# Writing out the gather and scatter loop of a mixture-of-experts kernel, with the scatter first in each step

## The reference

```python
x = x + attn(layernorm(x), w_qkv, w_out, decay_param)   # x: 2 x 1024 tokens of 512
x = x + ffn(layernorm(x), gate_w, w_gate, w_up, w_down, sw_gate, sw_up, sw_down)

# ffn: 8 experts of hidden size 352, two per token, and a shared expert of 704
scores = softmax(x @ gate_w)
topk_w, topk_idx = top_k(scores, 2)
routed = for each token: sum over its 2 experts of  topk_w * (silu(x @ w_gate[e]) * (x @ w_up[e])) @ w_down[e]
shared = silu(x @ sw_gate) * (x @ sw_up) @ sw_down
out = routed + shared
```

## Time and profile before

| what | us |
|---|---|
| median of 3 runs | 743.88 (741.69 to 747.67) |
| the profiled execution, its own time | 742.37 |
| its span, first to last instruction | 740.4 |
| PE busy in the span | 658.0 (89%) |
| DVE busy | 441.3 (60%) |
| ACT busy | 235.9 (32%) |
| POOL busy | 232.0 (31%) |
| mean granted PE clock | 0.967 |

### The profile page before, as it was taken

One profiled execution on the slowest core, in us unless ns is written; L12 is line 12 of the kernel. 1 busy time (PEld: TensorE's weight loads), 2 busy tenths in 40 slices (PEclk: granted clock), 3 DMA queues, 4 the chain that ended last, 5 costly groups with the idle time before them and its releaser, 6 DMA issues. The chain is left out here.

```text
span 740.4 us, 11819 instructions
## 1 busy us (share of the span) xinstructions
PE 658.0 (89%) x3677; PEld 424.2 (57%) x3678; DVE 441.3 (60%) x808; ACT 235.9 (32%) x353; POOL 232.0 (31%) x312
## 2 busy tenths in 40 slices
PE   3989889779899698899998999999999999999971
PEld 2757577558577365465655656655555555555540
DVE  6879878987997661687876976432333332233320
ACT  4244421242342222446665665411111111111110
POOL 6100110101102026333432343145444444443421
PEclk9999999999999899899999999999999999999995
DMA  6830012511342577875856315387986788897643
GB/s 214 289 116 15 15 30 72 163 37 45 113 100 78 129 192 198 263 178 150 182 150 147 57 29 86 61 138 130 114 133 128 121 122 115 121 124 128 106 66 42
DMA packets 111234, 86.86 MB, mean 117 GB/s; under 512 B 79280, under 2 KB 86448, under 8 KB 111200
## 3 DMA queue, kind: packets, MB, share of 16 engines
q1 hardware_dynamic: 88848, 43.94, 26.2%
q0 software_dynamic: 12272, 27.34, 22.9%
q10 hardware_dynamic: 10080, 15.14, 6.8%
HBM read 44.45 MB, written 23.33 MB: 92 GB/s over the span
## 5 line engine op out<-in xcount | busy, mean ns | idle before, releaser
L1298 DVE TENSOR_TENSOR hidT<-turn_h,hidT 128x384 f16<-128x384 f32 x71 | 39.4, 555 | 118.5 <-ACT hidT L1047 118.3
L381 PE MATMUL ring<-xnT_h,wq_h 128*128 128x512 f32 x192 | 81.1, 423 | 12.0 <-DVE run_kv L1208 5.2
L507 PE MATMUL ps_y<-routed,hidT 128*128 x351 | 84.0, 385 | 3.7 <-DVE hidT L1298 3.7
L507 PE MATMUL ps_g<-routed,x_in 128*128 x468 | 76.4, 313 | 11.0 <-issue 6.8
L1043 ACT ACTIVATE silu<-ps_g,job_silu 128x352 f32<-128x352 f32 x39 | 21.6, 554 | 202.3 <-PE ps_g L507 202.3
L839 POOL TENSOR_SCALAR var_eps<-mean_var 128x1 f32<-128x1 f32 x32 | 11.8, 369 | 227.0 <-DVE mean_var L1279 125.9
L381 PE MATMUL ring<-xnT_l,wq_h 128*128 128x512 f32 x192 | 78.4, 408 | 0.0
L381 PE MATMUL ring<-xnT_h,wq_l 128*128 128x512 f32 x192 | 78.2, 407 | 0.0
L507 PE MATMUL ps_u<-routed,x_in 128*128 x468 | 76.2, 313 | 0.0
L507 PE MATMUL ps_y<-shared,hidT 128*128 128x512 f16 x288 | 69.3, 387 | 7.6 <-DVE hidT L1298 7.6
L919 POOL DMA_INDIRECT out_dram<-y_job,idx_out x39 | 62.6, 1606 | 33.7 <-POOL idx_out L914 22.7
(11 more groups left out here) (224 smaller groups left out, 1105.7 us busy)
## 6 DMA issues: line engine op xcount, KB each, us to landing
routed<-in_L_ffn_w_gate_dram ACTq DMA_DIRECT2D x7, 704.0 KB, 4.9
routed<-in_L_ffn_w_up_dram ACTq DMA_DIRECT2D x7, 704.0 KB, 8.6
x_res<-in_L_attn_x_dram SPq DMA_DIRECT2D x18, 256.0 KB, 3.2
out_dram<-x SPq DMA_DIRECT2D x16, 256.0 KB, 3.4
xn_scratch<-xn_hl SPq DMA_DIRECT2D x16, 256.0 KB, 2.6
out_dram<-y_job POOLq DMA_DIRECT2D x16, 256.0 KB, 4.2
x_in<-in_L_attn_x_dram SPq DMA_DIRECT2D x14, 256.0 KB, 2.8
routed<-in_L_ffn_w_down_dram ACTq DMA_DIRECT2D x7, 512.0 KB, 10.9
```

Source lines behind the costliest of these rows:

```text
L381: ins = pe.matmul(ps, a, b, start=(i == 0), stop=(i == len(steps) - 1))
L507: ins = pe.matmul(ps, a[i][:, k, :], w(j, k), start=(start and q == 0), stop=(stop and q == len(steps) - 1))
L1298: dve.tensor_tensor(hidT[:, 1], turn_h[:, 0:FC, :], hidT[:, 0], ALU.subtract).then_inc(s["hidT_s"], 1)
```

## The change

The scatter and the gather are written out for every r, so r is a constant and `job_tok[:, r:r+1]` itself gives the row numbers. The buffers `idx_in` and `idx_out`, the 78 copies, their two semaphores and the register work go. The gather also waits for `xn2_out1` now, and no longer for its own last landing; the scatter no longer waits for `x2_out0`. The loop goes, and in each step scatter r stands ahead of gather r+4. In the queue, gather 4 stood ahead of scatter 0; it now stands behind it, and the same holds for every pair up to gather 38 and scatter 34.

```diff
-            def gather(r, b, first=False):
-
-                if not first:
-                    pool.wait_ge(s[f"gin{b}"], 8 * (r - b))
-                pool.tensor_copy(idx_in[:, b:b + 1], job_tok[:, bass.ds(r, 1)]).then_inc(s["idxg_s"], 1)
-                seen, free = pool.to_reg(r + 1), pool.to_reg(8 * (NT + r - b))
+            def gather(r):
+
+                b = r % 2
                 pool.wait_ge(s["xn2_out0"], 8 * NT)
-                pool.wait_ge(s["idxg_s"], seen)
-                pool.wait_ge(s[f"xin{b}"], free)
+                pool.wait_ge(s["xn2_out1"], 8 * NT)
+                if r >= 2:
+                    pool.wait_ge(s[f"xin{b}"], 8 * (NT + r - b))
                 pool.indirect_dma_start(x_job[:, b, :], None, xn2_d[:, :],
-                                        bass.IndirectOffsetOnAxis(idx_in[:, b:b + 1], 0))\
+                                        bass.IndirectOffsetOnAxis(job_tok[:, r:r + 1], 0))\
                     .then_inc(s[f"gin{b}"], 16)
 
-            def scatter(r, b):
-
+            def scatter(r):
+
+                b = r % 2
+                pool.wait_ge(s["y_s"], NT + r + 1)
                 pool.wait_ge(s[f"yo{1 - b}"], 16 * (NT // 2) + 8 * (r + b))
-                pool.tensor_copy(idx_out[:, b:b + 1], job_tok[:, bass.ds(r, 1)]).then_inc(s["idxs_s"], 1)
-                seen, ready = pool.to_reg(r + 1), pool.to_reg(NT + r + 1)
-                pool.wait_ge(s["x2_out0"], 8 * NT)
-                pool.wait_ge(s["idxs_s"], seen)
-                pool.wait_ge(s["y_s"], ready)
-                pool.indirect_dma_start(out[:, :], bass.IndirectOffsetOnAxis(idx_out[:, b:b + 1], 0),
+                pool.indirect_dma_start(out[:, :], bass.IndirectOffsetOnAxis(job_tok[:, r:r + 1], 0),
                                         y_job[:, b, :], None, compute_op=ALU.add).then_inc(s[f"yo{b}"], 16)
...
             for r in range(AHEAD):
-                gather(r, r % 2, first=r < 2)
+                gather(r)
...
-            with pool.Fori(0, (JOBS - AHEAD) // 2) as i:
-                for b in range(2):
-                    gather(2 * i + b + AHEAD, b)
-                    scatter(2 * i + b, b)
-            gather(JOBS - 1, 0)
-            for r in range(JOBS - AHEAD - 1, JOBS):
-                scatter(r, r % 2)
+            for r in range(JOBS):
+                scatter(r)
+                if r + AHEAD < JOBS:
+                    gather(r + AHEAD)
```

More of the change, by code:

```diff
@@ L218, in preln_decay_attention_moe @@
         job_y = msb("job_y", [P, JW])
-        idx_in = msb("idx_in", [P, 2], I32)
-        idx_out = msb("idx_out", [P, 2], I32)
         moe.close()
@@ L252, in preln_decay_attention_moe @@
             d_set d_route rt_exp rt_exp_in picked_s hot_s route_mm tables_s xin0 xin1 gin0
-            gin1 g_mm u_mm silu_s hid_s turned_h hidTh_s hidT_s y_mm y_s idxg_s
-            idxs_s yo0 yo1""".split()
+            gin1 g_mm u_mm silu_s hid_s turned_h hidTh_s hidT_s y_mm y_s yo0 yo1""".split()
         s = {n: sem(n) for n in names}
```

## The result

The changed kernel takes 739.26 us (median of 20 runs, 736.73 to 742.86), the kernel before in the same rounds 747.39 us (740.12 to 749.63). The ratio is 0.9903, with a 95% interval of 0.9882 to 0.9923: faster by 1.0%. All ratios here count, of each kernel, only the executions within 1.5% of its fastest one, so where the kernel before spreads widely a ratio can differ from the quotient of the medians. The profiled execution took 738.84 us with a span of 736.8 us, against 742.37 and 740.4 before.

A forecast was written before the change was run, and what follows sets the result against it. A chain of scatters, each landing before the next starts, bounds the jobs. Landing 5.55 plus restart 0.86 gives 6.41 us a step: -2.1 over 34 steps, -1.7 at the end, 742.37 to 738.6 us; range 730 to 748.

The forecast's parts named there:

- the sum: The jobs' scatter steps at 6.41 us, 34 of them saving 2.1 us, plus 1.7 after scatter 34: 738.6 us.
- What bounds it: In the jobs, from about 480 us on, each scatter must land before the next may start: 6.47 us a step.
- Term 1, the restart: Time from a scatter's landing to the next scatter's start: 0.86 us without the copy, against 1.13 to 1.24.
- The gathers' copies and the loop at nothing: Removing the 39 copies for gathers, the register work and the branches saves nothing, being hidden behind the scatter's landing.
- Term 2, the ring: PE's step, scatter, gather, transpose and back to PE now span three PE steps instead of four: 6.22 us a step.
- Term 3, the landing: A scatter takes 5.55 us to land, as transposes now start nearly with the next scatter; ends 5.0 and 5.9.
- The end: Scatters 34 to 38 take 23.5 us instead of 25.20, saving 1.7 us.
- What lies ahead, at nothing: The start, gathers 0 to 3 before scatter 0, moves nothing, as scatter 0 waits for the weighing.
- the restart is saved in full: Rival: in the scatter chain landings stay at 5.34 us, a step is 6.16, total 730.1 us; chance 0.25.

The follow-up runs named there:

- the repetition: The changed kernel run once more, unaltered, in later rounds against the kernel before: 739.31 us, ratio 0.9974.

## Why the prediction was right, point by point

Forecast 738.6 us, measured 739.26; the range and the side held. The mechanism held too, but that the number came within 0.7 us is in part luck. The size of the gain was 3.8 us by the sum and 8.1 us between the two medians. Between the two profiled executions it was 3.6 us, but not where the sum had it: 1.4 us in the 34 steps (2.1 forecast), 0.1 at the end (1.7 forecast), 2.3 ahead of scatter 0 (nothing forecast). The steps:

- *What bounds it.* Right: a chain of landings and restarts. The kernel with the gather first shows it: with the restart cut and the landings short, the time falls by 25 us and PE sets the pace.
- *Term 1, the restart.* 0.86 us was forecast and 0.77 came after a landing, 0.28 after a weighing. The step that failed is "the 0.8 us comes in front of an indirect DMA whatever it waited for". It depends on whether the wait stands ahead of the DMA or is carried by it, as the swapped waits show. In the kernel before, the wait for the weighing was the last of three written, so both rows used (scatters 0 and 16) had it standing ahead.
- *The gathers' copies and the loop at nothing.* Right: 722.22 us with the gathers' copies back, 742.50 with all back and the loop alone gone. A gather came 1.87 us behind its scatter and not 1.6.
- *Term 2, the ring.* Right that it moves beside the chain, at 6.22 against 6.41: 26 of 34 scatters were held by the landing and 5 by the weighing. Two of its parts missed in opposite ways. PE's part, from its step to the scatter, was 7.31 us (476.30 to 483.61) and not 7.90, because of the 0.28. The transpose and PE's wake were put at 4.0 us; over PE's 20 waits, from the transpose's start to PE's product, they took 4.9 us (median). The kernel with three ahead confirms the ring itself.
- *Term 3, the landing.* Right, and the term that decides: 5.55 forecast, a median of 5.7 measured; SP's wait always for a gather. Its cause was shown by taking the transposes away. The Trainium skill (DMA: Bandwidth & Descriptors, "Issuing engines are not separate DMA queues") says that DMAs run on the same 16 DMA engines and interleave, whichever engine started them; the 5.7 us beside a transpose against 4.8 us without one agree with that.
- *The sum.* 6.41 us a step forecast, 6.43 measured, and 6.51 in the profile of the repetition (482.34 to 703.59).
- *The end.* 23.5 us forecast for the scatters 34 to 38, 25.07 measured, so the upper bound of PE's 23 to 25 would have been the better choice. Scatter 35 (708.47) landed in 6.3 us, with a transpose 0.7 us behind it, and was followed by 36 at 715.50; the weighing held scatter 37 until 722.02.
- *What lies ahead, at nothing.* Scatter 0 started 2.28 us earlier. Of this 0.6 us is the cheap wait after the weighing (0.28 for 0.88), and 1.69 us lie ahead of the jobs: PE's gate product of job 1 stood at 477.99 and stands at 476.30. Nothing ties the 1.69 us to the change: among the profiles of the kernels with four gathers ahead scatter 0 starts anywhere from 482.3 to 486.7 us, and at 482.88 in the one that keeps loop and copies.
- *The size of the gain.* This is where the forecast fell short, in "I go by its own time". The profiled execution of before, 742.37 us, was a lucky one: the medians in four sets of rounds were 747.39, 745.98, 744.69 and 744.94. The steps of after were nearly right, and those of before were read off an execution 2 to 5 us below these medians. Had the sum started from 747.39 us, it would have given 743.6. No profile shows where the kernel before loses the rest. That before spreads over 734 to 750 us fits the mix of landings it shows, 5.0 in one stretch and 5.7 in another; the kernel with the gather first, which has almost only the short kind, spreads over 3.5 us. That the spread comes from this mix was not tested by itself.

What I did not see is the size of what the order costs. The rival "the restart is saved in full" was priced at 730.1 us with a landing of 5.34, the mean of before. The old order with the short restart is at 721. I had taken the mean landing for a property of the kernel. It is the mean of short and of long landings, and once the chain is faster than PE the long ones hardly come back: in the kernel with the gather first the landings from 485 to 706 us have a median of 4.8 us and a longest of 6.1.

## What to carry to other kernels

When transfers on several queues set the pace, ask which of them starts upon the landing of another, and whether that start falls on a transfer of the critical chain: here the same transposes cost 0.9 us a scatter at an offset near nothing and nothing at 2.7 us (at 1.9 to 2.3 us they mostly cost 1 us again). A change that shortens a chain and one that moves a queue's order should be timed apart, since this pair gained 1.0% together and 3.3% with the second left out. And a chain just above the pace of the engine it feeds is worth a small cut, for below that pace the waits that brought the transfers together can go away too, as they did here.

## What the runs showed of the hardware that was not expected

- An indirect DMA of POOL starts 0.28 us after a wait that it carries itself and 0.77 us after one that stands ahead of it as an instruction. Of two waits written before it, the first was the carried one. So the wait that is mostly fulfilled last is best written first; with the gather first that order took 721 us and the other 724, with the scatter first both took 739 to 740.
- A scatter of 256 KB with add landed in 4.4 to 5.1 us with no transpose about, and in 5.7 us (median) when one started with it. It took 5.9 to 6.2 us in eight of the twelve cases of the kernel before in which a transpose started 1.9 to 2.3 us behind it.
- Two kernels that differ by a copy of 0.18 us and its waits ahead of each of the 39 scatters (721 and, in five runs of six, 742 to 746 us) differ by 0.65 us a step (6.61 against 5.96, from the scatters 0 and 34 of their profiles): the landing, at 5.5 in place of 4.8, makes up most of it.
